# An attention block with NF4 feed-forward on one core: rotary products and masks moved from GpSimd and ScalarE to VectorE, half exchange by DMA

## What is computed

```python
x = x + attention(layernorm(x), ctx, ctx, mask)     # x (8,128,512), ctx (8,128,512)
#   32 query heads, 8 key/value heads of 128; q, k = rope(x Wq), rope(ctx Wk)
#   rope(x) = x * cos + rotate_half(x) * sin ;  rotate_half = (-x2, x1)
#   logits = 30 * tanh(q k * 0.0884 / 30);  masked softmax over T;  weights @ v;  @ Wo
x = x + (silu(n @ dq(w1).T) * (n @ dq(w2).T)) @ dq(w3).T      # n = layernorm(x)
#   dq: per block of 64, nearest of 16 code values times the block's largest absolute value
```

## Time and profile before

| | |
|---|---|
| median of 3 runs | 922.24 us (921.41 to 922.72) |
| the profiled execution, its own time | 921.3 us |
| its span in the profile | 919.3 us, mean granted TensorE clock 0.964 |
| instructions | 10659 |
| busy: PE, DVE, POOL, ACT | 823.1, 679.2, 634.7, 534.9 us |
| DMA | 70.83 MB, queue 1 busy 23.4% of 16 engines |
| chain that ended last | PE 53%, POOL 20%, DVE 17%, issue 5%, ACT 5% |

### The profile page before, as it was taken

How to read it: one execution, slowest core, us unless ns; L and a number is a source line. 1 busy time by engine, 2 the same in 40 slices (tenths; PEclk the granted TensorE clock), 3 DMA queues, 4 the chain that set the end, 5 groups by cost and what they waited for, 6 DMA issues and landing times.

```text
span 919.3 us, 10659 instructions
## 1 busy us (share of the span) xinstructions
PE 823.1 (90%) x3806; PEld 650.1 (71%) x3806; DVE 679.2 (74%) x793; ACT 534.9 (58%) x681; POOL 634.7 (69%) x352
## 2 busy tenths in 40 slices
PE   3688798799899899899899899899877899998998
PEld 2467585677677677677677677677555688887886
DVE  8999969487677677677677677687698789896120
ACT  1266478477588488577577577577554266463100
POOL 4778549899899898898898898898720334434000
PEclk9899899799999999999999999999899999999999
DMA  8213453311311311312312212211200310403210
GB/s 315 98 51 115 146 181 108 104 35 46 121 35 47 120 35 49 118 35 56 110 35 70 98 37 82 83 45 44 78 0 32 101 46 3 153 1 100 55 58 35
DMA packets 49140, 70.83 MB, mean 77 GB/s; under 512 B 4160, under 2 KB 25792, under 8 KB 49088
## 3 DMA queue, kind: packets, MB, share of 16 engines
q1 hardware_dynamic: 49088, 70.15, 23.4%
HBM read 51.00 MB, written 19.14 MB: 76 GB/s over the span
## 4 chain that ended last, share of the span: by engine, by line
PE 53%; POOL 20%; DVE 17%; issue 5%; ACT 5%; DMA 0%; POOLq 0%; DVEq 0%; SPq 0%; ACTq 0%
POOL qT L1085 6%; DVE nfa L807 4%; PE bank L397 4%; PE bank L395 4%; PE bank L396 4%; PE bank L415 4%; PE bank L414 4%; PE bank L413 4%; POOL sw L1081 4%; PE bank L429 4%; PE avp L493 4%; PE bank L431 4%; PE bank L430 4%; PE bank L482 3%; PE trp L402 3%
## 5 line engine op out<-in xcount | busy, mean ns | idle before, releaser
L807 DVE SCALAR_TENSOR_TENSOR nfa<-nfp,nfa 128x1408 f32<-128x1408 uint8 x168 | 326.6, 1944 | 99.8 <-ACT nfp L624 98.6
L624 ACT ACTIVATE nfp<-nfv,bnd 128x1408 uint8<-128x1408 f32 x180 | 256.0, 1460 | 61.5 <-POOL nfv L1103 51.1
L1085 POOL TENSOR_TENSOR qT<-qT,sw 128x512 f32<-128x512 f32 x80 | 165.3, 2066 | 34.9 <-DVE qT L814 25.1
L631 ACT ACTIVATE sw<-bank 64x512 f32<-64x512 f32 x80 | 47.5, 594 | 139.5 <-PE bank L415 93.1
L429 PE MATMUL bank<-woh,ath 128*128 128x512 f32 x256 | 110.5, 432 | 0.0
L413 PE MATMUL bank<-xh,wqh 128*128 128x512 f32 x256 | 107.9, 422 | 0.0
L1137 POOL TENSOR_TENSOR eb<-eb,maskf 128x512 f32<-128x512 f32 x64 | 92.6, 1448 | 17.8 <-ACT eb L686 17.8
L431 PE MATMUL bank<-woh,atl 128*128 128x512 f32 x256 | 104.4, 408 | 0.0
L430 PE MATMUL bank<-wol,ath 128*128 128x512 f32 x256 | 104.3, 407 | 0.0
L414 PE MATMUL bank<-xl,wqh 128*128 128x512 f32 x256 | 103.0, 402 | 0.0
L415 PE MATMUL bank<-xh,wql 128*128 128x512 f32 x256 | 103.0, 402 | 0.0
(11 more groups left out here) (120 smaller groups left out, 1664.9 us busy)
## 6 DMA issues: line engine op xcount, KB each, us to landing
dq_scratch<-nfa SPq DMA_DIRECT2D x12, 704.0 KB, 3.1
stage<-wq_pieces SPq DMA_DIRECT2D x32, 256.0 KB, 2.9
stage<-wo_pieces SPq DMA_DIRECT2D x32, 256.0 KB, 2.6
stage<-dq_scratch SPq DMA_DIRECT2D x32, 256.0 KB, 3.2
nfv<-nf_rest SPq DMA_DIRECT2D x7, 704.0 KB, 4.1
ks_scratch<-qT SPq DMA_DIRECT2D x16, 256.0 KB, 2.1
vs_scratch<-vst SPq DMA_DIRECT2D x16, 256.0 KB, 2.4
kcur<-ks_scratch SPq DMA_DIRECT2D x16, 256.0 KB, 2.9
```

The lines of the kernel that those rows point to most:

```text
L624: nc.scalar.activation(nfp[:, i % 2, :], nfv[:, :], ACT.Sign, bias=bnd[:, i:i + 1])\
L807: op = nc.vector.scalar_tensor_tensor(nfa[:, :], nfp[:, b % 2, :], STEPS[b], nfa[:, :], ALU.mult, ALU.add)
L1085: nc.gpsimd.tensor_tensor(dst, dst, sw[:, slot, :], ALU.add).then_inc(roped, 1)
```

## The change

It moves the whole of both rotary products to DVE: one instruction (`rope_parts`) reads the bank once and writes both `x*cos` and `x*sin` (128 x 1024) to a new pair of buffers, `cs_start` for the key units and the first six query units, `cs_loop` for the rest. The half exchange is then made on the sine product, by two DMAs of SP (`swap`, 64 partitions each, one semaphore per slot), and the sign of the sine table is turned round for it. POOL only adds. ACT's two copies are gone. The mask product goes to DVE (`mask(j + 2)` behind `atl` of step `j`) and reads the logits' bank, in which tanh and exp now stay; so logits `j` wait for `weights_done` and no longer for `tanh_done`. Waits that stood before a write of `qT` go with it from DVE to POOL. The diff, cut to its core:

```diff
+        def products(ru, slot):
+            return (cs_start if ru < NK + AHEAD else cs_loop)[:, slot, :, :]
@@ SP
+            def swap(ru, slot):
+                sp.wait_ge(cs_done, ru + 1)
+                wait(sp, roped, ru - 1)
+                part = products(ru, slot)
+                sp.dma_start(sw[0:64, slot, :], part[64:128, 1, :]).then_inc(swapped[slot], 16)
+                sp.dma_start(sw[64:128, slot, :], part[0:64, 1, :]).then_inc(swapped[slot], 16)
...
             nf_load(nf_first[:, 0:CH], 0)
+            swap(0, 0)
+            swap(1, 1)
...
-            for u in range(8):
-                k_store(u)
...
+            k_store(0)
+            for u in range(2, NK):
+                swap(u, u % 2)
+                k_store(u - 1)
...
@@ PE: q_unit(u), logits(j)
-                wait(pe, cos_done, NK + u - 1)
+                wait(pe, cs_done, NK + u - 1)
...
-                wait(pe, tanh_done, j)
+                wait(pe, weights_done, j)
@@ ACT
-            def swap(ru, slot):
-                act.wait_ge(proj_done, ru + 1)
-                wait(act, roped, ru - 1)
-                nc.scalar.activation(sw[0:64, slot, :], prj[slot][64:128, :], ACT.Copy)
-                nc.scalar.activation(sw[64:128, slot, :], prj[slot][0:64, :], ACT.Copy).then_inc(swapped, 1)
...
-                nc.scalar.activation(eb[:, j % 2, :], lgp[:, :], ACT.Tanh, scale=MULT / CAP).then_inc(tanh_done, 1)
+                nc.scalar.activation(lgp[:, :], lgp[:, :], ACT.Tanh, scale=MULT / CAP).then_inc(tanh_done, 1)
...
-                nc.scalar.activation(eb[:, j % 2, :], eb[:, j % 2, :], ACT.Exp, scale=CAP).then_inc(exp_done, 1)
+                nc.scalar.activation(lgp[:, :], lgp[:, :], ACT.Exp, scale=CAP).then_inc(exp_done, 1)
@@ DVE
-            def cos_part(ru, slot, dst, cos):
-                dve.wait_ge(swapped, ru + 1)
...
+            def rope_parts(ru, slot, both):
+                dve.wait_ge(proj_done, ru + 1)
+                wait(dve, roped, ru - 1)
+                nc.vector.tensor_tensor(
+                    products(ru, slot).rearrange("p c (b t) -> p c b t", b=4),
+                    prj[slot][:, :].rearrange("p (o b t) -> p o b t", o=1, b=4).to_broadcast([128, 2, 4, S]),
+                    both.rearrange("p c (o t) -> p c o t", o=1).to_broadcast([128, 2, 4, S]), ALU.mult)\
+                    .then_inc(cs_done, 1)
...
+            def mask(j):
+                dve.wait_ge(exp_done, j + 1)
+                wait(dve, av_done, j - 1)
+                nc.vector.tensor_tensor(eb[:, j % 2, :].rearrange("p (g t) -> p g t", g=G),
+                                        lgp[:, :].rearrange("p (g t) -> p g t", g=G),
+                                        maskf[:, :].rearrange("p (o t) -> p o t", o=1).to_broadcast([128, G, S]),
+                                        ALU.mult).then_inc(weights_done, 1)
@@ POOL
-                pool.wait_ge(swapped, ru + 1)
-                part = sw[:, slot, :].rearrange("p (b t) -> p b t", b=4)
-                nc.gpsimd.tensor_tensor(part, part, sin.rearrange("p (o t) -> p o t", o=1).to_broadcast([128, 4, S]),
-                                        ALU.mult).then_inc(sin_done, 1)
-                pool.wait_ge(cos_done, ru + 1)
-                pool.wait_ge(sin_done, ru + 1)
-                nc.gpsimd.tensor_tensor(dst, dst, sw[:, slot, :], ALU.add).then_inc(roped, 1)
+                pool.wait_ge(cs_done, ru + 1)
+                pool.wait_ge(swapped[slot], 32 * (ru // 2 + 1))
+                nc.gpsimd.tensor_tensor(dst, products(ru, slot)[:, 0, :], sw[:, slot, :], ALU.add).then_inc(roped, 1)
```

124 lines of the change are left out of this document (62 added, 62 removed).

## The result

| | before | changed |
|---|---|---|
| median | 922.49 us (921.41 to 923.17, 6 runs) | 915.09 us (911.93 to 917.95, 6 runs) |
| ratio of the two | | 0.9926, 95% interval 0.9913 to 0.9939 |
| the profiled execution, span | 919.3 us | 912.9 us (its own time 914.74) |

What follows compares the result with a forecast made beforehand. PE, busy 90%, was taken as the bound, with a ring through PE, ACT and DVE almost without slack, and DVE bounding the key phase. Sum: 921.3 - 2 + 2 - 10.2 - 7.5 = 903.6, forecast 904 us, range 888 to 924.

Steps and rivals of the forecast that it cites:

- last head: Last head: four masks on the chain cost +2.4 us, its own change gives about as much back, sum 0.
- key phase: Before the heads: 16 double products on DVE cost +8.5 us, fewer stretched DVE instructions give -10.5, net -2.
- start of the heads: First head: without the swap the first value product starts at 159.0, not 166.00; with a later qT wait, -7.5 us.
- quiet steps: Five or six of a head's eight steps: +0.07 us a step in some 35 ring-bound steps, +2 us.
- six changes: From head to head: no PE wait for mask or qT left, -1.7 us for each of six, -10.2 us.
- The ring: Quiet step's loop of PE's logits, ACT, DVE and PE's next-step transposes: 8.60 us, to become 8.74.
- The first rival: Exchange halves land one after the other, 4.2 us not 2.6, the add 1.6 later: 920, or 924 to 928; chance 0.10.
- those for a right forecast: No PE wait on POOL at changes, two on DVE (2.7 us), value product near 159, POOL 50%, DVE 80%, quiet step 7.74-7.85.
- those for a wrong one: PE waiting for POOL's add at b=2 or b=6, swaps after 3.5 us, table steps over 1.9, steps above 8.2, value phase after 105.
- Nothing moves: A slower DVE eats the start's gain and head changes stay at 6.2 us: 921; chance 0.05.
- key phase pays: Before the heads, DVE's stretches move to adds and lows instead of going: +8.5 to +10 us, 913; chance 0.17.
- PE keeps its pace: At a head's change the slow output products (4.43 against 2.88 us) go, -1.55 x 7: 893; chance 0.12.

Runs made afterwards that it cites:

- e4: Changed kernel without its 116 exchange transfers, POOL adding the two products as they lie (rotation left out): 904.63 us, ratio to before 0.9823.
- e5: Changed kernel with DVE's rotary double product moved right behind nrm, ahead of the table steps: 897.66 us, ratio to before 0.9740.
- e9: Changed kernel with POOL's power moved ahead of the third key unit's rotary add in the key phase: 912.17 us, ratio to before 0.9897.
- e6: Changed kernel with the third table chunk's load ahead of keys, values and three weight pieces: 912.96 us, ratio to before 0.9903.
- e2: Kernel before with only the mask product moved to DVE, the sine product staying on POOL: 914.08 us, ratio to before 0.9931.
- e1: Rotary half of the change alone, the mask staying on POOL with tanh and exp in eb as before: 919.08 us, ratio to before 0.9980.
- e13: Changed kernel with the last head's masks back on POOL: 915.13 us, ratio to before 0.9928.
- e7: Changed kernel with one transfer of 128 partitions in place of two of 64, halves not exchanged: 900.65 us, ratio to before 0.9775.
- e14: Changed kernel with the second half of each exchange issued by POOL, the first by SP: 990.59 us, ratio to before 1.0741.

## Why the prediction was right and wrong

The step that failed is the price of the exchange. The prediction gave it 2.6 us, compared that with the logits that need the unit's `qT`, found 0.4 us of margin and charged nothing. It charged nothing either for what else waits behind POOL's add, and it put the last head at 0 without the exchange. The runs showed 3.06 us from product to add, and behind the add the power in the key phase (3.98 us of DVE's time) and the scaling at each change (2.7 us late). The last head cost 4.5 us, in part for reasons that stay open. Leaving the exchange out gives 10 us (e4), and starting it earlier gives 17 (e5). A second step failed at the start of the heads, where a table load came late out of SP's queue (3.73 us).

By the forecast's own steps, with the measured value from the logits products of the two profiled executions:

| step | forecast | measured |
|---|---|---|
| key phase, to the first logits product | -2 | -0.6 |
| start of the heads, to the fifth | -7.5 | -4.4 |
| quiet steps | +2 | +2.8 |
| six changes | -10.2 | -8.7 |
| last head | 0 | +4.5 |
| sum | -17.7 | -6.4 |

- **Key phase: sum wrong by 1.4, one term right, one too small, one missing.** The 16 double products took 19.4 us where the cosine products had taken 10.9, the +8.5 of the forecast. The rest of DVE's work up to 102 us fell by 15.6 and not by 10.5, so that its busy time went from 95.0 to 87.9, with 7 us to spare where I had 2. But waits that I had not walked through took them: 3.98 us for POOL's power (1.2 before), behind an add, behind an exchange, behind four weight pieces on SP's queue; 3.7 us for adds that hold DVE's two product buffers; and 2.2 for a weight piece. I had written that POOL's `low` pieces there are wanted tens of us later, and had not asked for whom else the queue stood. e9 shows the first of these waits; e4 gives 5 us for all of the exchange up to here. The -0.6 itself is no better known than to 1 us.
- **Start: the first part right, the next wait missed.** The second logits product was forecast at 158 and came at 158.07, the first value product at 159.0 and came at 159.88. Behind it the reduction waited 3.73 us for a load that SP issued at 159.90. I had checked this load's margin at a head's change, 1.5 us, and not here, where three weight pieces, keys and values stand in front of it (e6).
- **Quiet steps: right size, wrong cause, so luck.** The ring of 8.74 us never bound: the step is 7.74. The 2.8 us are `qT` waits at `b` = 6 (up to 0.55) and the slower steps around them. I had given the add a margin of 0.4 us. It was over by 0.46 of exchange (3.06 against 2.6) and 0.66 of a table step stretched by `low`. The first rival thus came true in small: not two landings but a second issue, and the part that decided was not in it at all.
- **Changes: right size, one wait of two.** From the second to the fifth product a change is 1.5 to 1.7 us shorter in five of the six, against 1.7, with the mask's wait of 1.85 on DVE; the sixth gave 0.7, for its `qT` wait of 1.44. "No wait for mask or `qT` is left" was wrong: the `qT` waits are there in five of six. In the walked-through change (from 350.48 in the changed kernel) the last add ends at 30.46 and not at 29.3 to 29.9. Its output products kept their pace (2.8 us and not 4.4), and PE waits 0.78 us for that add, so the logits come at the forecast's 30.5 by two errors that cancel; in the changes with slow output products they come at 30.6 or 30.7, or at 31.5 with the wait of 1.44. What I missed besides is what stood beside it: I let POOL's scaling end "at 16.4 as today" and took this for no cost. It was the 2.7 us behind the add, and e5 took most of it.
- **Last head: the largest miss, +4.5 for 0.** The +2.4 for masks was added up and offset against its own change, and the exchange was left out of it. Without a query product from `b` = 2 on the logits want the last `qT` at once, and the wait for it grew from 1.48 to 3.05. The chain behind it is in-order ACT and DVE. Shown is, from the second product of the last head to the middle of the feed-forward part, that an earlier double product brings the 4.5 down to 1.0 (e5), that mask or rotary part alone give 1.0 and 1.5 (e2 and e1), that 3.9 stay without any exchange (e4), and that moving the masks back does not help (7.3 in e13's long execution). So neither part makes the 4.5 by itself, and how they arise from the two together is open.
- **The signs.** Of those for a right forecast, the waits for mask and `nrm`, DVE's share and the first value product came. Of those for a wrong one, one came: PE waiting for POOL's add at `b` = 2 and `b` = 6.
- **The rivals.** "Nothing moves" and "key phase pays" did not occur; the latter's sum should have been 914 and not 913 (+8.5 in place of -2). "PE keeps its pace" came true in two of the six changes and brought nothing. There the output products take 2.8 us, where they take 3.3 to 4.3 in the other four, and PE then waits 0.29 us for `nrm` and 0.77 for `qT`: from the second to the fifth product are 27.6 us in the two, and 27.7 to 27.8 in three of the four. Only with `qT` early, in e5, is the pace worth 1.1 us a change. Where the slow stretch comes, it is short: behind the wait at 564.20 PE's granted clock is 0.82 over the step and 1.00 in the windows around it, with 0.57 and 0.43 us from start to start for the first two output products and 0.23 to 0.27 for the others (columns as in the earlier trace rows).

```profile
554.50:564.20 9.70, 7.85 (x39) 5.88 (x37) 8.49 (x8) 4.90 (x6) 1.47 (x2) 1.00 0.20 37
564.20:573.70 9.50, 9.50 (x39) 7.16 (x39) 6.63 (x12) 2.25 (x4) 6.94 (x4) 0.82 0.63 221
573.70:583.00 9.30, 7.90 (x39) 5.98 (x37) 8.28 (x10) 6.21 (x8) 5.11 (x5) 1.00 0.44 119
```

## What to carry to other kernels

When work that an engine did itself becomes a product, a transfer and an add, the question is not what the transfer occupies but what waits behind the add: every instruction queued there inherits the transfer's latency. Start such a transfer at the first place where its input exists, even ahead of work that was first in line (17 us here), and count its issues: a second one cost 14 us here, in a kernel whose single transfer left the exchange out, so whether the exchange itself can be had with one issue is not shown. A margin of 0.4 us in a forecast is none: add up what each neighbour can stretch before calling it free.

## What the hardware showed that I had not expected

- 64 partitions (128 KB) and 128 partitions (256 KB) between SBUF and SBUF both land 2.3 us after issue; the price of a second half is mostly SP's 0.5 us of issue, and without it the kernel was 14 us shorter (e7).
- A half issued by POOL landed 3.2 us after its issue where SP's took 2.2 (medians in e14), and left late where POOL was busy; with 80 of them the kernel was 75 us longer.
- A delay can protect: without any exchange the add falls on DVE's table step, which takes 2.54 us instead of 1.61, and the kernel is 7 us slower than with the product moved forward and the exchange kept (e4 and e5).
- A wait that comes later can hide what an earlier one costs: at full pace (2.8 us for twelve output products) and at a granted clock of 0.64 (4.3 us) a change of the changed kernel is equally long (27.6 and 27.7 us from the second to the fifth product), since at full pace PE waits for `nrm` and `qT` instead.
